# ScalarE's exponential of the next pair ahead of the last eviction in each attention slot

## What is computed

```python
def _L1_attn_ref(x, Wq, Wk, Wv, Wo, bo):
    Q = (x @ Wq.T).reshape(B, T, H, D).transpose(0, 2, 1, 3)
    K = (x @ Wk.T).reshape(B, T, H, D).transpose(0, 2, 1, 3)
    V = (x @ Wv.T).reshape(B, T, H, D).transpose(0, 2, 1, 3)
    scores = jnp.einsum('bhqd,bhkd->bhqk', Q, K) / jnp.sqrt(jnp.float32(D))
    causal = jnp.tril(jnp.ones((T, T), dtype=bool))
    scores = jnp.where(causal, scores, -jnp.inf)
    weights = jax.nn.softmax(scores, axis=-1)
    out = jnp.einsum('bhqk,bhkd->bhqd', weights, V)
    out = out.transpose(0, 2, 1, 3).reshape(B, T, C)
    return out @ Wo.T + bo
```

## Time and profile before

| | us |
|---|---|
| median of 3 runs | 1243.29 (1242.9 to 1245.18) |
| profiled execution, its own time | 1245.89 |
| its span, first to last instruction | 1244.0 |
| TensorE matmul busy | 1078.6 (87% of the span) |
| TensorE weight load busy | 913.4 (73%) |
| ScalarE busy | 631.2 (51%) |
| VectorE busy | 616.9 (50%) |
| GpSimd busy | 396.8 (32%) |
| mean granted TensorE clock | 0.951 |

### The profile page before, as it was taken

How to read it: one execution, slowest core, us unless ns; L and a number is a source line. 1 busy time by engine, 2 the same in 40 slices (tenths; PEclk the granted TensorE clock), 3 DMA queues, 4 the chain that set the end, 5 groups by cost and what they waited for, 6 DMA issues and landing times.

```text
span 1244.0 us, 27330 instructions
## 1 busy us (share of the span) xinstructions
PE 1078.6 (87%) x9892; PEld 913.4 (73%) x9893; DVE 616.9 (50%) x1174; ACT 631.2 (51%) x1067; POOL 396.8 (32%) x272
## 2 busy tenths in 40 slices
PE   6988888879988886999999999990578888869998
PEld 5877777767766664888888888880467777659998
DVE  3236665553332324566666666650156666624443
ACT  3446666643443432555555555550276566635554
POOL 2143434414544433012222222211456555341110
PEclk9999999988998988999999999995689999989999
DMA  6550000044111113011111111103100000000000
GB/s 226 186 216 2 2 0 1 3 162 151 27 23 23 24 20 93 22 34 34 34 34 34 34 34 34 33 27 98 56 27 28 33 1 2 3 1 21 16 13 30
DMA packets 30806, 57.25 MB, mean 46 GB/s; under 512 B 12892, under 2 KB 22314, under 8 KB 29588
## 3 DMA queue, kind: packets, MB, share of 16 engines
q1 hardware_dynamic: 16184, 44.06, 10.2%
q0 software_dynamic: 13328, 10.66, 3.3%
q10 hardware_dynamic: 1228, 1.61, 0.4%
HBM read 41.52 MB, written 14.67 MB: 45 GB/s over the span
## 4 chain that ended last, share of the span: by engine, by line
PE 68%; POOL 9%; ACT 9%; issue 8%; DMA 3%; DVE 2%; SPq 0%; ACTq 0%; POOLq 0%; DVEq 0%
PE ps L1193 22%; PE ps L1198 12%; PE ps L1200 11%; PE ps L1199 11%; POOL routed_in L458 6%; PE ps L1312 5%; ACT prs L610 2%; PE ps L1304 2%; PE ps L1569 2%; ACT vts L603 2%; DMA yg<-routed_out 1%; POOL xn L389 1%; ACT QT L598 1%; PE ps L1552 1%; ACT lnv L568 1%
## 5 line engine op out<-in xcount | busy, mean ns | idle before, releaser
L482 POOL DMA_INDIRECT routed_out<-yt,tile_to x43 | 65.7, 1528 | 290.4 <-DVE yt L1128 290.4
L1106 DVE TENSOR_TENSOR tile_w<-arena,tile_w 128x1408 fp32r<-128x1408 f32 x86 | 139.3, 1621 | 36.1 <-ACT tile_w L782 36.1
L1193 PE MATMUL ps<-arena,shared 128*128 x516 | 130.9, 395 | 1.0 <-ACT shared L778 1.0
L1198 PE MATMUL ps<-tile_w,xTs 128*128 128x352 f32 x344 | 120.0, 349 | 3.0 <-DVE xTs L1111 3.0
L782 ACT ACTIVATE tile_w<-arena 128x1408 fp32r x86 | 118.3, 1377 | 7.5 <-issue 7.5
L945 DVE TENSOR_TENSOR Hd<-Sg,ps 128x296 f32<-128x296 f32 x96 | 44.4, 462 | 148.5 <-ACT Sg L723 139.7
L771 ACT ACTIVATE shared<-ps 128x352 f32<-128x352 f32 x86 | 40.0, 465 | 145.7 <-PE ps L1200 141.2
L1200 PE MATMUL ps<-tile_w,xTs 128*128 128x352 f32 x344 | 112.1, 326 | 0.0
L1199 PE MATMUL ps<-tile_w,xTs 128*128 128x352 f32 x344 | 111.8, 325 | 0.0
L1193 PEld LDWEIGHTS ps<-arena,shared 128*128 128x128 f32 x516 | 90.8, 189 | 27.9 <-issue 15.6
L1193 PE MATMUL ps<-xn,shared 128*128 128x296 f32 x352 | 108.6, 455 | 0.0
(11 more groups left out here) (196 smaller groups left out, 2701.4 us busy)
## 6 DMA issues: line engine op xcount, KB each, us to landing
arena<-in_ew_dram SPq DMA_DIRECT2D x7, 2176.0 KB
x_in<-in_xT_dram SPq DMA_DIRECT2D x7, 888.0 KB, 4.9
xt<-routed_in SPq DMA_DIRECT2D x43, 129.0 KB, 2.0
yg<-routed_out SPq DMA_DIRECT2D x8, 592.0 KB
out_dram<-h SPq DMA_DIRECT2D x8, 296.0 KB, 2.7
routed_in<-zero_x SPq DMA_DIRECT2D x13, 129.0 KB, 10.5
gu_i<-in_gu_dram SPq DMA_DIRECT2D x1, 1536.0 KB, 20.9
shared<-in_gu_dram SPq DMA_DIRECT2D x1, 1408.0 KB, 7.4
```

The source lines that it names most:

```text
L482: pool.indirect_dma_start(ys, bass.IndirectOffsetOnAxis(tile_to[b][:, 0:1], 0), yt[b][:], None).then_inc(s_yt, 16)
L1106: dve.tensor_tensor(tile_w[half][1], gate_up_of(w, half), tile_w[half][0].bitcast(F32), ALU.subtract).then_inc(s.wl, 1)
L1193: return pe.matmul(out_, lhsT, rhs, start=start, stop=stop)
L1198: pe.matmul(out_, w[1], x[0], start=start, stop=False)
```

## The change

On ScalarE alone, in each of the four slots, the exponential of the next pair is issued before the last eviction of the slot and no longer after it. No instruction is added or removed in what it computes, and the order on the other engines is the same.

```diff
--- before.py
+++ after.py
@@ -673,8 +673,9 @@
                         dequantise_gate_up()
                     if not X.last:
                         project(g + 1, 0, X.bank("proj0"))
+                    exps(n + 1, 1)
+                    if not X.last:
                         project(g + 1, 1, X.bank("proj1"))
-                    exps(n + 1, 1)
 
                     shares(n, 0, X.bank("O0"))
                     probs_t(n + 1, 1)
@@ -683,8 +684,9 @@
                     if not X.last:
                         project(g + 1, 2, X.bank("proj2"))
                         squares(*norm_ahead(l, g, X))
+                    exps(n + 2, 2)
+                    if not X.last:
                         project(g + 1, 3, X.bank("proj3"))
-                    exps(n + 2, 2)
 
                     shares(n + 1, 1, X.bank("O1"))
                     probs_t(n + 2, 2)
@@ -692,8 +694,9 @@
                         dequantise_down()
                     if not X.last:
                         deviation(*norm_ahead(l, g, X), X.bank("var"))
+                    exps(n + 3, 3)
+                    if not X.last:
                         project(g + 1, 4, X.bank("proj4"))
-                    exps(n + 3, 3)
 
                     shares(n + 2, 2, X.bank("O2"))
                     probs_t(n + 3, 3)
@@ -704,8 +707,8 @@
                             upper_x(a, g + 2, b, xa[b])
                         elif l == 1:
                             upper_x(F[1], 0, 0, xf1[0])
+                        exps(n + 4, 0)
                         project(g + 1, 5, X.bank("proj5"))
-                        exps(n + 4, 0)
                 over_body(act, l, step)
                 shares(4 * GROUPS - 1, 3, last.bank("O3"))
                 upper_out(GROUPS - 1, 1)
```

## The result

| | before | with the change |
|---|---|---|
| median of 3 runs, us | 1243.29 | 1258.23 |
| lowest and highest | 1242.9, 1245.18 | 1251.35, 1263.65 |
| ratio (95% interval) | | 1.0109 (1.0081 to 1.0136) |
| span of the profiled execution | 1244.0 | 1261.8 |
| mean granted TensorE clock | 0.951 | 0.926 |

The change makes the kernel slower by 1.1%, where I forecast 3.1 us less. The three runs lie further apart than those of before, and they differ in the clock: 1263.65 us at a mean of 0.926, 1258.23 at 0.927, 1251.35 at 0.935. From here on, lines of kernel.py behind 710 are three higher than in the rows of before: L1315 for L1312, L1307 for L1304, L1196 for L1193, L855 for L852.

What follows compares the result with a forecast made beforehand. An attention group was taken to be bounded by TensorE and its gaps waiting for ScalarE. Layer 0's -2.95 and layer 1's -0.14 gave -3.1 us, from 1243.29 to 1240.2 us, range 1227 to 1247.

Steps and rivals of the forecast that it cites:

- Slots 1 to 3: Stretches between successive pairs' probability transposes: the earlier exponential saves 0.75, 0.39 and 0.97 us in layer 0.
- slot 3: Exponential starts right behind the norm's Exp, ahead of the value eviction: -0.97 us.
- slot 1: Exponential ahead of the second KT eviction: -0.75 us in layer 0 (0.29 from earlier projection loads), -0.46 in layer 1.
- Slot 2: Exponential takes the QT eviction's place, 0.39 us earlier, and TensorE follows: -0.39 us.
- Slot 4: Exponential waits for DVE's centring, held by POOL's subtraction, delaying the eviction and V0n: +1.98 us.
- rival A: In slot 4 DVE's centring starts before POOL's subtraction; slots 3 and 4 give -0.14, not +1.01: 1227.5 us, chance 0.17.
- Group 6 of layer 0: No POOL subtraction in slot 4, centring 0.77: slots 3 and 4 give -0.25, with slots 1 and 2 -1.4.
- The sum of the order: Both attention stages, all groups: -2.95 us in layer 0, -0.14 in layer 1, together -3.1.
- rival B: TensorE's clock falls in the longer wait before V0n, 1.0 us eleven times: +8, 1251 us, chance 0.10.
- The range: Whole kernel: 1227 to 1247 us, taking in rival A and the forecast with its bounds.
- being wrong in the large: A layer 0 group, 23.97 us before, coming out shorter than 23.2 or longer than 24.5 us.

Runs made afterwards that it cites:

- e7_slots_1_2: The change in slots 1 and 2 only, against the kernel before: 1234.49 us, ratio 0.9912.
- e6_slot_3: The change in slot 3 only, against the kernel before: 1236.65 us, ratio 0.9922.
- e2_slot_4: The change in slot 4 only, slots 1 to 3 as in the kernel before: 1266.97 us, ratio 1.0176 against it.
- e8_filled_half: The whole change plus two unread matmuls on TensorE in the wait before V0n, against the kernel before: 1238.84 us, ratio 0.9946.
- e4_upper_last: The whole change, with ScalarE's upper_x moved behind the eviction in slot 4, against the kernel before: 1235.59 us, ratio 0.9921.
- e1: The change in slots 1 to 3 without slot 4, against the kernel before: 1227.94 us, ratio 0.985.
- e3_filled: The whole change plus four unread matmuls on TensorE in the wait before V0n, against the kernel before: 1241.99 us, ratio 0.9964.

## Why the prediction was wrong, point by point

- **Slots 1 to 3.** Right in layer 0: forecast -0.75, -0.39, -0.97; measured -0.90, -0.39, -0.98 at a clock of 1.00. In layer 1 slot 3 is right and slot 1 gained 0.59 where I took 0.46; where the 0.1 beyond the idle of 0.49 comes from isn't shown. Slot 2 of layer 1 is wrong: forecast -0.39, measured +0.03 to +0.06 in groups 1 to 4. The centring was free there in the kernel before (0.77 us). Now POOL's sum of routed rows (L494) starts ahead of it and the mask of keys (L379) follows, the centring takes 2.74, and the exponential waits for it. From group 1 of the changed kernel:

```profile
946.74 2.36 POOL L494 TENSOR_TENSOR yg<-yg 74x1024 f32<-74x1024 f32 x1
...
948.14 2.74 DVE L855 TENSOR_TENSOR Sb<-Sb,mx 128x592 f32<-128x592 f32 x1
...
950.91 0.70 ACT L610 ACTIVATE prs<-Sb 128x592 f32<-128x592 f32 x1 [0.32 <-DVE Sb L855]
```

  This slot is 6.31 us in e7_slots_1_2 too, and 6.27 as before in e6_slot_3: it comes with the shorter slot 1, not with slots 3 and 4.
- **Slot 4.** Right in mechanism and size: +1.98 forecast, +1.8 to +2.25 measured, by the centring that waits for POOL, the exponential that waits for it, and the eviction behind both. The race that rival A rests on was lost as forecast, in all eleven groups (0.15 us forecast, 0.16 measured), though DVE had won it in three of them before. Group 6 of layer 0 was to have no collision and to gain 1.4; there the centring takes 1.46, behind POOL's mask of keys, and the group gains 0.9 at a clock of 1.00.
- **The sum of the order.** Right to within about 1 us: for groups 1 to 7 the steps give -2.65 in layer 0 and +0.36 in layer 1, and the traces at 1.00 show -3.6 and +0.3. In layer 1 that is partly luck, since the error in slot 2 (1.7 us in four groups) is made up by slots 1 and 4. The medians, -3.9 and -7.5, say no more than that it is a small gain.
- **The step that failed** is the one that let TensorE's work behind V0n run at the granted clock of the earlier trace rows. I had seen that the wait would be 2.5 us and had put this down as rival B with a chance of 0.10, on the ground that the one long wait in the rows, 3.61 us, came after a sparse stretch. That it came after one was no evidence that a wait in a dense stretch is harmless; the rows had waits of 1.24 at 1.00 and nothing between that and 3.61, and I put nine tenths on the better side of that gap. The trace of before had a case inside it, which I passed over. The longest of the 50 waits of the earlier trace rows, 2.17 us, stands ahead of the first slot of group 0 of layer 0. In the 12.02 us up to 76.02 TensorE had been busy for 10.32 at 1.00, in the next 3.46, with that wait, for 1.28, and the slot that follows has a mean of 0.74 (the stretches have the columns of the earlier trace rows):

```profile
79.48 1.10 PE L1312 MATMUL ps<-cst,prs 128*74 128x128 f32 x8 [2.17 <-ACT prs L610]
```

```profile
64.00:76.02 12.02, 10.32 (x78) 9.15 (x78) 1.54 (x2) 6.24 (x13) 5.06 (x4) 1.00 0.70 277
76.02:79.48 3.46, 1.28 (x20) 0.79 (x21) 3.37 (x4) 1.23 (x2) 2.85 (x2) 1.00 1.07 458
79.48:86.08 6.60, 6.11 (x88) 5.00 (x89) 3.40 (x5) 2.32 (x5) 1.89 (x3) 0.74 0.64 272
```

  Rival B was right, in its place and nearly in its price: I had 1.0 us for each of eleven groups and a total of 1251; measured were 1.6 on average in ten of fourteen in the slowest run, and a median of 1258. The clock falls by half for a part of the next slot. My 0.84 was a mean over 4 us of which 1.6 were idle and which end inside the low stretch, so it made the price too small.
- **The range** (1227 to 1247) left rival B out, and that is where the time fell. One case on the other side with a price of 11 us should have been inside it or should have had its chance worked out from what the trace could not exclude. Groups 2, 4 and 5 of layer 0 took 24.8, 25.9 and 25.3 us, over the 24.5 that I had named as being wrong in the large.
- The Trainium skill (TensorE: Matmul & The Clock Gate, HAM oscillation) describes matmul bursts that are cut apart by waits for DMA and each start cold. The traces agree for waits on ScalarE: the slot behind ran partly at 1.2 GHz in 6 of 9 cases at 2.0 us (e2_slot_4) and in 9 of 12 at 2.5 (changed kernel), and in none at about 1.3.

## What to carry to other kernels

Before an instruction is put ahead of another on an in-order engine, ask for each pair which of the two is waited for last, slot by slot: the same edit was worth 18 us in three slots and cost more than that in the fourth, since there the eviction was the late one and the exponential waited for a third engine. And when a change lengthens one wait of TensorE, price the clock as well as the wait: a wait longer than any that the trace shows at full clock is an unknown with a price of its own, and it can be tested for by filling it with matmuls that nobody reads.

## What the runs showed of the hardware

- TensorE's clock fell to 1.2 GHz behind single waits inside a stretch in which it was otherwise busy for almost nine tenths of the time. Waits of 1.15 to 1.38 us before V0n, 23 of them in e8_filled_half and e4_upper_last, were followed by no stretched slot; those of 1.83 to 2.08 in the changed kernel and in e1, e4 and e6 by one in 3 of 7 cases; waits of 2.0 us (e2_slot_4) in 6 of 9; those of 2.43 to 2.56 (changed kernel) in 9 of 12. The 2.17 us ahead of the first slot of layer 0 were followed by one (means of 0.58 to 0.78) in nine of the ten kernels. Like waits don't always have it. That would account for the 12 us between the three runs of the changed kernel, but only one of them has a trace.
- More work for TensorE made the kernel faster: eight fp32 matmul passes for each group, 2.26 us of them, took 18.9 us off groups 1 to 7 of the two attention stages (trace of e3_filled against that of the changed kernel's slowest run).
- A DVE subtraction with both inputs in SBUF took 0.76 us alone and 1.93 when a POOL subtraction had started 0.16 us before it. Where the DVE one started 0.06 us ahead, it took 0.77 and the POOL one 2.03 instead of 1.45.
